# Fourteen extra idle products on TensorE ahead of the third batch's first transposes

## The reference, cut to what matters

```python
xn = layernorm(x)
x = x + L0_attn(xn) + L0_ffn(xn)   # elu+1 linear attention (cumulative sum over tokens); top-32 of 512 "genes"
xn = layernorm(x)
x = x + L1_attn(xn) + L1_ffn(xn)   # sigmoid(q) * cumsum(exp(k) v) / cumsum(exp(k)), then swiglu; 16 experts, top 2, and a shared one
```

```python
xn = x * rsqrt(mean(x * x) + eps) * norm_w
logits = einsum('btd,gd->btg', xn, Wc) / clip(temperature, 0.1)
top_vals, top_idx = top_k(logits, 32)
```

## Time and profile before

| what | before |
|---|---|
| time, median of 3 executions (lowest to highest) | 546.76 us (545.47 to 547.53) |
| the profiled execution's own time | 545.26 us |
| its span, first to last instruction | 543.5 us |
| granted TensorE clock, mean over the span | 0.985 of full |
| PE busy | 505.8 us, 93% |
| DVE busy | 358.6 us, 66% |
| ACT busy | 293.7 us, 54% |
| POOL busy | 275.8 us, 51% |

### The profile page before, as it was taken

The page is one execution under the profiler, slowest core; times in us unless marked ns, Lnnn a source line. Parts: engine busy times, 40 slices in busy tenths (PEclk is TensorE's granted clock), DMA queues, the critical chain, the costliest instruction groups (busy, mean ns, idle before and its releaser), DMA issues.

```text
span 543.5 us, 7472 instructions
## 1 busy us (share of the span) xinstructions
PE 505.8 (93%) x2480; PEld 383.8 (71%) x2480; DVE 358.6 (66%) x734; ACT 293.7 (54%) x575; POOL 275.8 (51%) x207
## 2 busy tenths in 40 slices
PE   8987999859999999999987999899999999999993
PEld 5544577646777865768966888777777777777882
DVE  4999987867998679967799979323233242323356
ACT  4868788557877578977573542333334333333220
POOL 0545546636726714473254492646667665563200
PEclk9999999989999999999999999999999999999996
DMA  8800040020302000031700759422232223222148
GB/s 288 343 2 1 1 154 2 39 77 2 138 18 87 30 9 32 0 156 62 261 1 0 239 199 297 113 60 85 81 114 82 68 78 137 87 74 64 39 180 295
DMA packets 19765, 54.27 MB, mean 100 GB/s; under 512 B 3312, under 2 KB 5744, under 8 KB 19728
## 3 DMA queue, kind: packets, MB, share of 16 engines
q1 hardware_dynamic: 15216, 41.47, 21.9%
q0 software_dynamic: 4512, 12.33, 7.7%
HBM read 36.09 MB, written 17.70 MB: 99 GB/s over the span
## 4 chain that ended last, share of the span: by engine, by line
PE 67%; DVE 15%; ACT 7%; DMA 4%; issue 3%; POOL 2%; SPq 1%; DVEq 0%; POOLq 0%; ACTq 0%
PE bank L275 46%; PE bank L437 9%; PE bank L350 2%; PE bank L496 2%; PE bank L469 2%; DMA y_rows<-m_y,dest 1%; DMA ga<-y_rows 1%; DVE fe L1025 1%; PE bank L357 1%; DVE tk L968 1%; DVE bn L872 1%; PE bank L339 1%; DMA xg<-xn_rows,tab 1%; DMA w_vec<-in_vec 1%; DVE m L966 1%
## 5 line engine op out<-in xcount | busy, mean ns | idle before, releaser
L1208 DVE TENSOR_TENSOR m_h<-m_h,bank 128x176 f32<-128x176 f32 x47 | 15.9, 338 | 93.9 <-ACT m_h L784 93.9
L1359 POOL DMA_INDIRECT y_rows<-m_y,dest x47 | 46.6, 992 | 52.8 <-DMA y_rows<-m_y,dest 29.0
L275 PE MATMUL bank<-mw,m_xt 128*128 x188 | 65.4, 470 | 0.9 <-issue 0.9
L275 PE MATMUL bank<-yhr,wsg_h 128*128 128x512 f32 x128 | 56.1, 438 | 3.3 <-DVE hs L1084 1.7
L1350 POOL DMA_INDIRECT xg<-xn_rows,tab x47 | 46.1, 981 | 20.1 <-issue 9.2
L275 PE MATMUL bank<-hyr,wsg_h 128*128 128x512 f32 x128 | 50.2, 392 | 0.0
L275 PE MATMUL bank<-yhr,wsg_l 128*128 128x512 f32 x128 | 50.1, 392 | 0.0
L275 PE MATMUL bank<-mw,m_ht 88*128 x188 | 48.4, 379 | 0.0
L275 PE MATMUL bank<-fe,w_qkv 128*128 128x512 f32 x96 | 44.5, 595 | 1.9 <-ACT fc L646 1.9
L275 PEld LDWEIGHTS bank<-mw,m_ht 88*128 88x128 f32 x188 | 35.3, 190 | 11.2 <-issue 0.3
L275 PEld LDWEIGHTS bank<-mw,m_xt 128*128 128x128 f32 x188 | 32.3, 190 | 14.2 <-issue 2.5
(11 more groups left out here) (240 smaller groups left out, 1427.1 us busy)
## 6 DMA issues: line engine op xcount, KB each, us to landing
mw<-in_gu SPq DMA_DIRECT2D x16, 352.0 KB
ga<-y_rows SPq DMA_DIRECT2D x8, 512.0 KB, 7.3
mw<-in_dn SPq DMA_DIRECT2D x16, 176.0 KB
wsg_w<-in_wsg SPq DMA_DIRECT2D x4, 512.0 KB, 14.3
spilled_r<-fb SPq DMA_DIRECT2D x4, 512.0 KB, 3.2
spilled_x<-fa SPq DMA_DIRECT2D x4, 512.0 KB, 2.7
xn_rows<-fg SPq DMA_DIRECT2D x4, 512.0 KB, 3.3
hx<-spilled_x SPq DMA_DIRECT2D x4, 512.0 KB, 4.7
```

The source lines that it names most:

```text
L275: mm = e.matmul(o, a, b, start=n == 0, stop=n == len(terms) - 1)
L1208: e.tensor_tensor(m_h[j % 3][:, :], m_h[j % 3][:, :], ps("ju", j)[:, 176:352], ALU.mult).then_inc(s["jh"], 1)
L1359: e.indirect_dma_start(out=y_d, out_offset=bass.IndirectOffsetOnAxis(ap=dest[:, j:j + 1], axis=0), in_=m_y[j % 3][:, :], in_offset=None).t ...
```

## The change

`awake` gets a second argument, the bank that it writes, with bank 6 as the default; it now waits for that bank's last reader. One new call, `awake(14, 2)`, stands between `ddown(0, 1, 6, 7)` and `turn1(2, 0, 2)`: fourteen products into bank 2, the bank that `turn1` takes next. All other calls, on every engine, are as they were.

```diff
-            def awake(n):
+            def awake(k, n=6):
 
                 q.wait_ge(s["wdr"], 1)
-                o = banks.t[6]
-                for _ in range(n):
+                if banks.back[n]:
+                    q.wait_ge(*banks.back[n])
+                o = banks.t[n]
+                for _ in range(k):
                     e.matmul(o[:, 0:D].rearrange("p (k t) -> p k t", t=P), still[:, :], still[:, None, :].broadcast_to([P, 2, P]), start=True, stop=True)
...
-            dup(0, 1, 0); dgate(0, 2, 1); ddown(0, 0, 6, 7); dup(0, 2, 5); oproj(1, 1, 4); ddown(0, 1, 6, 7); turn1(2, 0, 2); turnr(1, 0, 1)
+            dup(0, 1, 0); dgate(0, 2, 1); ddown(0, 0, 6, 7); dup(0, 2, 5); oproj(1, 1, 4); ddown(0, 1, 6, 7); awake(14, 2); turn1(2, 0, 2); turnr(1, 0, 1)
```

## The result

| | before | changed |
|---|---|---|
| median, and the span of its executions | 546.53 us (545.47 to 547.53, six) | 543.03 us (541.3 to 543.47, six) |
| ratio, 95% interval | 1 | 0.9932 (0.9913 to 0.9952) |
| profiled execution: own time, span, clock | 545.26, 543.5, 0.985 | 543.38, 541.6, 0.990 |

The change makes the kernel 3.5 us faster. I had forecast 1.6 us, "within 0.5%", and a range down to 543.7. The two profiled executions differ by only 1.9 us.

A forecast was written before the change was run, and what follows sets the result against it. PE, busy 505.8 of 543.5 us, was taken to bound the kernel. 2.09 us from the high clock less 0.45 of later start gave 1.64, so 546.76 - 1.6 = 545.2 us, range 543.7 to 547.3, "within 0.5%".

The forecast's parts named there:

- The local sum: From `turn1(2, 0)` to `qproj2(1, 0)`: 2.09 us shorter at the high clock, less 0.45 of later start, 1.64 us gained.
- overrun: At `turn1(2, 0)`: the fourteen products end at 120.89, past the old start of 120.44, a loss of 0.45 us.
- What was late next: Behind the stretch, the chain's detours to ACT and DVE move with PE; 0.8 to 1.64 us arrive, whole taken.
- Rival 2: Behind the stretch, another chain, such as DVE's backlog from 275 to 307, keeps the gain: 546.0 to 547.2 us; chance 0.17.
- Rivals 1 and 3: In the gap: clock falls anyway, 546.8 or 547.2 to 547.5 us, chance 0.07; products run at half pace, 553.2, chance 0.03.
- The rule: For the idle products: matmul distance N / 2.4 + 2.5 ns, so 0.109 us per record; the forecast used the trace's 0.216.
- rival 4: More gain than the sum, from a longer low stretch or a closed DVE pause; hardly over 3 us, 543.8; chance 0.10.
- clock term: Gain from TensorE's clock staying at 1.00 behind the gap ahead of `turn1(2, 0)`, forecast as 1.64 us net.
- Two clock readings: Idle stretches at 28.4 to 30.9 (2.41 us) and 280.3 to 282.7 (2.35 us) leave PE's clock at 1.00.

The follow-up runs named there:

- the gap alone: A separate kernel without the computation, repeating a 5.1 us idle gap 66 times with six fillings; with nothing 7.09 us, with the clock kept 5.08 us.
- e15: Against before: 56 instructions of already met waits in the gap ahead of `turn1(2, 0)`, plus ten idle products ahead of the last `ddown`; 543.89 us, ratio 0.9954.
- e10: Against before: 56 instructions of already met waits in the gap ahead of `turn1(2, 0)`, no idle products; 545.24 us, ratio 0.9954.

## Why the prediction was wrong in size

**The local sum was right.** Fourteen products of 0.216 us (6.04 measured, 6.05 forecast) cost an overrun of 0.48 (forecast 0.45, as twelve against fourteen shows); the clock stays at 1.00; L296 starts at 120.75 and not 120.9, MAX8 at 124.22. At the same mark the profiles are 1.7 us apart, the sum said 1.64. Against the profiled execution's own time I forecast 543.6 us and the profiled execution of the changed kernel took 543.38. On one chip, with the shift held equal, the timed executions give 1.4, and the gap alone 2.0 - 0.45 = 1.55.

**What was late next: nothing.** The gain passes from 127.6 to 325 without loss: in 16 of the 17 profiles of this kernel and its versions the stage takes 197.4 to 197.5 us, before's three among them. Only e15's, at 198.2, is outside. From 325 to 519.9 the profiles scatter too much to follow 1.6 us (194.6 to 194.8 us in before's three, 194.4 to 198.7 in the others); there the timed executions speak, 1.4 us on one chip. Rival 2 didn't happen, and taking the whole and not a part was right.

**Rivals 1 and 3.** Products of a constant tile do hold the clock, if they are wide: the narrow ones don't. The clock was up when they started, as in the earlier trace rows, so they ran at full pace.

**The rule.** The 28 records take 0.216 us each in this trace as in the earlier trace rows. The estimate of 0.109 us worked out from the Trainium skill, "TensorE: Matmul & The Clock Gate", section "Back-to-back issue gap", doesn't fit a float32 record.

**The step that failed** is the bound of rival 4 and the sentence that "Nothing else moved": I counted an added instruction by its time on the array alone. It also takes a place in PE's instruction stream. That term is missing from the sum, and it is about as large as the one that I had: 0.9954 and 0.9970 for 56 idle instructions, their middle 0.9962, or 2.1 us, and 0.9966 for the narrow products. With the clock term of 1.64 us (0.9970) the product is 0.9932, what was measured; with intervals of 0.002 to either side, agreement to the last digit is luck. So the whole came to 543.03 us, below the 543.7 at which my range ended. The limit "hardly more than 3 us can come" looked only at the gap, while what can be located of the gain beyond came 400 us later. The rows to warn me were there: in before's chain the last two scatters, of the same size, land after 3.01 and 4.69 us, and the page counts 21 instruction packets.

**How much of it is explained.** In all three profiles of before a fetch starts 1.7 to 1.8 us behind the issue of the last scatter and takes 0.96 to 1.76 us, and the scatter lands at 3.82 to 4.69 us. In each of the three, two 4 KB packets of the scatter start just as the fetch ends (3.54, 2.67 and 2.93 us behind the issue; the fetch ends at 3.55, 2.68 and 2.94), while the scatter's others are through by 2.2 us, and the landing follows 0.47 us behind the last packet. In the fourteen profiles of the other kernels the nearest fetch starts 0.6 us behind the issue or earlier, and SP goes on 3.25 to 3.3 us behind it. So the traces show that the fetch delays the landing. The last stage then takes 18.0 to 19.0 us and not 19.4 to 20.2. The late landing itself is 0.6 to 1.5 us of the 2, and less where another chain ends last, as in e10. The rest, about 1 us, isn't located, and what it is stays open: 14 and 28 instructions free the scatter too and gain 0.3 and 0.8 us by their ratios. The intervals, 1 us to either side, are as wide as what would have to be split.

**Two clock readings were chance.** I wrote that idle stretches of 2.41 and 2.35 us leave the clock up. In the first repeat of before it is down at 30.8 to 34.3, behind the same gap, and in the changed kernel's profile at 32.1 to 35.5 and 281.3 to 284.7. The same gap drops it in one execution and not in the next. The forecast didn't hang on them. They do explain why one profile isn't the median.

## What to carry to other kernels

Price an added or removed instruction twice: by its time on the engine, and by the shift that it gives to the fetches behind it in the engine's instruction stream. The second can't be forecast from the number of instructions; test it by adding the same number of waits that are already met, at the same place. Fill a long idle gap of TensorE with wide products that end just ahead of the awaited input: twelve did what fourteen did, without the overrun, and narrow ones didn't hold the clock. Read a clock dip in several executions before you price it, and a DMA on the last chain by what else its trace shows in the same microseconds.

## What was unexpected of the hardware

- Instruction fetches show as 16 KB packets on a queue of their own, 21 in the run, each 0.9 to 1.8 us in before's profile. Three times in three the small scatter that one met landed after 3.8 to 4.7 us and not 3.24, because two of its packets started only when the fetch had ended.
- 56 instructions without any work, in a gap in which the engine waits anyway, made a 546 us program 0.30 to 0.46% faster.
- 28 float32 records of 8 columns take 0.107 us each and don't hold the clock: low behind the gap in 12 of 12 passages. Records of 256 columns hold it with 12 products in 11 of 11.
- In the kernel of the gap alone the same gap costs between 1.2 and 2.9 us from one passage to the next, with the clock low for 3.4 or 6.8 us. Seven wide products, with 2.1 us of idle time left, held it in 4 passages of 11.
